# A convolution attention's weighted sums from 16-bit halves, with the rests made on GpSimd and VectorE

## The reference, cut to what is touched

```python
k = conv1x1(xA, wk, bk)      # (4, 128, 1024); v and q alike
attn = softmax(einsum('bcn,bcm->bnm', v, q), axis=2)
av = einsum('bcn,bnm->bcm', k, attn)
avw = einsum('oc,bcn->bon', wwg, av)
avw = (avw - bn1_m) * scale1 + bn1_b
o = conv1x1(avw, wout, bout)
o = (o - bn2_m) * scale2 + bn2_b
x = relu(o + xA)
# then: t = tokens(x); t += attention(layernorm(t)); t += experts(layernorm(t))
```

## Time and profile before

| | us |
|---|---|
| median of 3 runs | 1248.38 (1245.92 to 1252.49) |
| the profiled execution's own time | 1251.72 |
| its span, first to last instruction | 1249.9 |
| TensorE busy | 1120.8 (90%) |
| VectorE, ScalarE, GpSimd busy | 794.2, 634.3, 577.8 |
| granted TensorE clock, mean | 0.961 |

### The profile page before, as it was taken

How to read it: one execution, slowest core, us unless ns; L and a number is a source line. 1 busy time by engine, 2 the same in 40 slices (tenths; PEclk the granted TensorE clock), 3 DMA queues, 4 the chain that set the end, 5 groups by cost and what they waited for, 6 DMA issues and landing times.

```text
span 1249.9 us, 28738 instructions
## 1 busy us (share of the span) xinstructions
PE 1120.8 (90%) x10344; PEld 739.8 (59%) x10344; DVE 794.2 (64%) x1458; ACT 634.3 (51%) x1147; POOL 577.8 (46%) x461
## 2 busy tenths in 40 slices
PE   3999999975799999899989998689899999999993
PEld 1555555533344554454445444578799989998772
DVE  2666666655788888678768872666566555555540
ACT  0757575742477668666765675433233333333432
POOL 2425242413488761675276337256454444454420
PEclk9999999977799999999999999799999999999996
DMA  5235852544022230333243214623333233332228
GB/s 164 63 114 185 317 187 80 186 130 146 27 74 78 83 78 27 96 95 95 63 109 88 57 45 127 251 36 71 51 50 47 47 49 51 53 52 40 41 31 273
DMA packets 98854, 120.50 MB, mean 96 GB/s; under 512 B 29120, under 2 KB 76032, under 8 KB 98080
## 3 DMA queue, kind: packets, MB, share of 16 engines
q1 hardware_dynamic: 77744, 70.15, 19.0%
q0 software_dynamic: 20544, 42.22, 15.2%
q10 hardware_dynamic: 432, 6.29, 1.3%
HBM read 72.84 MB, written 45.60 MB: 95 GB/s over the span
## 4 chain that ended last, share of the span: by engine, by line
PE 80%; DVE 5%; DMA 4%; ACT 3%; issue 3%; SPq 1%; DVEq 1%; another core or an unknown queue 0%; POOL 0%; ACTq 0%; POOLq 0%
PE PP L945 25%; PE PP L1313 14%; PE PP L1201 9%; PE PP L1175 9%; PE PP L1029 4%; PE PP L1080 4%; PE PP L1126 3%; PE PP L1185 3%; PE PP L1190 2%; DVE mxp L1539 2%; PE PP L977 2%; DMA WB<-late_d 2%; ACT WB L872 1%; PE PP L1054 1%; PE PP L1280 1%
## 5 line engine op out<-in xcount | busy, mean ns | idle before, releaser
L872 ACT ACTIVATE WB<-PP 128x512 f32<-128x512 f32 x512 | 268.4, 604 | 174.8 <-PE PP L1201 174.8
L1539 DVE TENSOR_REDUCE mxp<-PP 128x2 f32<-128x1024 f32 x256 | 301.3, 1219 | 66.0 <-PE PP L1126 64.4
L916 ACT ACTIVATE WORK<-PP,b1c 128x256 f32<-128x256 f32 (+1 forms) x320 | 142.4, 450 | 266.0 <-PE PP L945 248.5
L945 PE MATMUL PP<-WORK,WB 128*128 128x256 f16 (+2 forms) x1984 | 221.1, 268 | 18.1 <-issue 9.7
L672 POOL TENSOR_TENSOR WB<-WB 128x1024 f32<-128x1024 f32 x80 | 188.9, 2361 | 78.2 <-PE PP L1190 69.4
L945 PEld LDWEIGHTS PP<-WORK,WB 128*128 (+1 forms) x1984 | 186.1, 103 | 49.2 <-issue 21.4
L728 POOL DMA_INDIRECT res_d<-WORK,lb x71 | 116.1, 1635 | 200.1 <-DVE WORK L1779 180.2
L1313 PE MATMUL PP<-WB,WORK 128*128 x1704 | 194.9, 273 | 0.0
L1313 PEld LDWEIGHTS PP<-WB,WORK 128*128 128x128 f16 x1704 | 164.4, 98 | 22.0 <-issue 0.9
L1201 PE MATMUL PP<-WORK 97*128 97x256 f16 x1024 | 159.3, 279 | 16.0 <-ACT WB L872 12.9
L638 POOL TENSOR_TENSOR WB<-WORK,WB 128x1024 f16<-128x1024 f32 x32 | 68.4, 2137 | 174.0 <-ACT WORK L778 173.9
(11 more groups left out here) (287 smaller groups left out, 1144.0 us busy)
## 6 DMA issues: line engine op xcount, KB each, us to landing
WORK<-in_L_ffn_W_dram POOLq DMA_DIRECT2D x32, 512.0 KB, 4.3
res_d<-WORK SPq DMA_DIRECT2D x8, 1024.0 KB, 4.5
late_d<-WB POOLq DMA_DIRECT2D x1, 6144.0 KB, 19.1
WB<-late_d ACTq DMA_DIRECT2D x3, 2048.0 KB, 14.8
v_d<-WORK SPq DMA_DIRECT2D x4, 1024.0 KB, 4.5
WORK<-q_hi_d SPq DMA_DIRECT2D x16, 256.0 KB, 3.6
WORK<-v_d SPq DMA_DIRECT2D x8, 512.0 KB, 5.8
WORK<-k_hi_d SPq DMA_DIRECT2D x16, 256.0 KB, 3.9
```

The source lines that it names most:

```text
L872: act.activation(PR[n % 3][:, c // 2, c % 2 * 2:c % 2 * 2 + 2], SCORES[m % 3] .rearrange("p (h n) -> p h n", h=2), ACT.Exp).then_inc(s("e_ ...
L916: act.activation(hid[:, k, 0:width], hidden_bank(k)[:, 0:width], ACT.Gelu, bias=b1c[:, bass.ds(e, 1), k], scale=1.0 / WSCALE)\
L945: mm = pe.matmul(dst, lhsT, rhs, start=(n == 0), stop=(n == len(pairs) - 1))
L1539: dve.tensor_reduce(mxp[:, n // 4 % 2, i, h:h + 2, k], PP[2 + h // 2][:, :].rearrange("p (h n) -> p h n", h=2), X_AXIS, ALU.max).then_inc( ...
```

## The change

- The exponential goes to `expo[i % 2]` in 32 bits. ScalarE waits for its own result and copies it to a 16-bit high half in `prob[i % 4][:, 0]` (semaphore hi_on). The rest, `expo - high`, goes to `prob[i % 4][:, 1]`: GpSimd makes it for blocks 0, 1, 2, 4, 5, 6, VectorE for 3 and 7.
- exp(i) waits for the rest of block i - 2; in batches 1 to 3 exp(0) also waits for the batch before's q and k stores to land.
- VectorE scales the row sum by 1/256, inverts it, makes the keys' high half and (scalar_tensor_tensor) their low half. S1 takes the 1/256 back.
- weigh(i) is three 16-bit products for each half of the columns instead of one 32-bit product, and waits for the rest.
- The weights: ScalarE splits part 0 after block 2, part 1 after block 7, parts 2 and 3 ahead of the layer norm's halves, and parts 4 to 7 after the units 0 to 3. GpSimd makes the rests of blocks 0 to 2 ahead of part 0's low half and those of 4 to 6 ahead of part 1's.

```diff
+KSCALE = 256.0
+REST_BY_VECTOR = (3, 7)
...
+        halved = "p (s n) -> p s n"
+        prob = [a.bitcast(F16).rearrange(halved, s=2) for a in prob]
...
+        expo = [QS[:, i * N:(i + 1) * N] for i in range(2)]
...
+            def low_exponentials(b, i):
+                pool.wait_ge(s("hi_on"), b * NT + i + 1)
+                if i >= 4:
+                    pool.wait_ge(s("av_made"), b * NT + (i - 3))
+                pool.tensor_tensor(prob[i % 4][:, 1], expo[i % 2], prob[i % 4][:, 0], ALU.subtract)\
+                    .then_inc(s("lo_pool"), 1)
+
             for i, (e, _, at, gap) in enumerate(parts):
+                for k in {0: (0, 1, 2), 1: (4, 5, 6)}.get(i % 8, ()):
+                    low_exponentials(i // 8, k)
...
             def tokens(b, last):
+                def rests(n):
+                    late = sum(i <= n for i in REST_BY_VECTOR)
+                    act.wait_ge(s("lo_pool"), b * (NT - 2) + n + 1 - late)
+                    if late or b:
+                        act.wait_ge(s("lo_dve"), b * 2 + late)
+
+                if b:
+                    act.wait_ge(s("st_q0"), FREE + b * 64)
+                    act.wait_ge(s("st_q1"), FREE + b * 64)
                 for i in range(NT):
                     act.wait_ge(s("max_kept"), b * NT + (i + 1))
+                    if i >= 2:
+                        rests(i - 2)
+                    act.activation(expo[i % 2], PP[i % 3][:, :], ACT.Exp, bias=nmax[:, i:i + 1],
+                                   accum_out=rsum[:, i:i + 1]).then_inc(s("exp_kept"), 1)
                     if i >= 4:
                         act.wait_ge(s("av_made"), b * NT + (i - 3))
-                    act.activation(prob[i % 4], PP[i % 3][:, :], ACT.Exp, bias=nmax[:, i:i + 1],
-                                   accum_out=rsum[:, i:i + 1]).then_inc(s("exp_kept"), 1)
-                    if i % 2 == 0:
-                        split_weights(b, i // 2)
-                split_weights(b, 4)
+                    act.wait_ge(s("exp_kept"), b * NT + i + 1)
+                    act.activation(prob[i % 4][:, 0], expo[i % 2], ACT.Copy).then_inc(s("hi_on"), 1)
+                    if i == 2:
+                        split_weights(b, 0)
+                split_weights(b, 1)
...
-                split_weights(b, 5)
+                split_weights(b, 2)
+                split_weights(b, 3)
...
-                    if u < 2:
-                        split_weights(b, 6 + u)
+                    split_weights(b, 4 + u)
...
                 def weigh(i):
-                    pe.wait_ge(s("exp_kept"), b * NT + (i + 1))
+                    pe.wait_ge(s("hi_on"), b * NT + (i + 1))
                     pe.wait_ge(s("ks_kept"), b * NT + (i + 1))
+                    if i in REST_BY_VECTOR:
+                        pe.wait_ge(s("lo_dve"), b * 2 + REST_BY_VECTOR.index(i) + 1)
+                    else:
+                        pe.wait_ge(s("lo_pool"), b * (NT - 2) + i + 1 - (i > 3))
...
                     for h in range(2):
-                        mm = pe.matmul(PP[3][:, h * HALF:(h + 1) * HALF], kTs[i % 4],
-                                       prob[i % 4][:, h * HALF:(h + 1) * HALF],
-                                       start=(i == 0), stop=(i == NT - 1))
+                        here = slice(h * HALF, (h + 1) * HALF)
+                        for n, (sk, sp) in enumerate(((0, 0), (0, 1), (1, 0))):
+                            mm = pe.matmul(PP[3][:, here], kTs[i % 4][:, sk], prob[i % 4][:, sp, here],
+                                           start=(i + n == 0), stop=(i == NT - 1 and n == 2))
...
                     dve.wait_ge(s("exp_kept"), b * NT + (i + 1))
+                    dve.tensor_scalar(rsum[:, i:i + 1], rsum[:, i:i + 1], 1.0 / KSCALE, None, ALU.mult)
+                    dve.drain()
                     dve.reciprocal(rinv[:, i:i + 1], rsum[:, i:i + 1])
...
-                    dve.tensor_scalar(kTs[i % 4], kT[:, i * P:(i + 1) * P], rinv[:, i:i + 1], None,
-                                      ALU.mult).then_inc(s("ks_kept"), 1)
+                    key = kT[:, i * P:(i + 1) * P]
+                    dve.tensor_scalar(kTs[i % 4][:, 0], key, rinv[:, i:i + 1], None, ALU.mult)
+                    dve.drain()
+                    dve.scalar_tensor_tensor(out=kTs[i % 4][:, 1], in0=key, scalar=rinv[:, i:i + 1],
+                                             in1=kTs[i % 4][:, 0], op0=ALU.mult, op1=ALU.subtract)\
+                       .then_inc(s("ks_kept"), 1)
+                    if i in REST_BY_VECTOR:
+                        dve.wait_ge(s("hi_on"), b * NT + i + 1)
+                        dve.tensor_tensor(prob[i % 4][:, 1], expo[i % 2], prob[i % 4][:, 0], ALU.subtract)\
+                           .then_inc(s("lo_dve"), 1)
```

More of the change, by code:

```diff
@@ L205, in hybrid_block @@
         qs = QS.bitcast(F16).rearrange("p (u s n) -> p u s n", u=2, s=2)
+        expo = [QS[:, i * N:(i + 1) * N] for i in range(2)]
         stage = take(2048).rearrange("p (u n) -> p u n", u=2)
-        kTs = [take(P) for _ in range(3)] + [SPARE[:, 3 * N:3 * N + P]]
+        kTs = [a.bitcast(F16).rearrange(halved, s=2)
+               for a in [take(P) for _ in range(3)] + [SPARE[:, 3 * N:3 * N + P]]]
         wqkv16 = take(1536).bitcast(F16).rearrange("p (s c n) -> p s c n", s=2, c=CC)
@@ L325, in s @@
             return S[name]
-        for name in ("q_low v_low ld_w ld_x0 ld_x1 ld_y0 ld_y1 bst_kept pool_const pe_prep dve_prep act_prep "
+        for name in ("q_low v_low ld_w ld_x0 ld_x1 ld_y0 ld_y1 bst_kept hi_on lo_pool lo_dve pool_const pe_prep dve_prep act_prep "
                      "q_made v_made k_made q_kept v_kept k_kept sc_made max_kept exp_kept ks_kept "
@@ L1394, in _ @@
             dve.tensor_tensor(vec[:, BE2:BE2 + 2], vec[:, BO:BO + 2], vec[:, BB2:BB2 + 2], ALU.add)
+            dve.tensor_scalar(vec[:, S1:S1 + 1], vec[:, S1:S1 + 1], 1.0 / KSCALE, None, ALU.mult)
             dve.wait_ge(s("pe_prep"), 2)
```

## The result

The changed kernel takes 1325.2 us in the median of four runs (1322.1 to 1327.7), the kernel before on the same chip 1249.1 (1245.9 to 1252.5): a ratio of 1.060, 95% interval 1.057 to 1.063, so it is 76 us slower. The direction was forecast; the time is 20 us above the 1305 and 3 us beyond the range.

The account below looks back on a forecast made before the run. TensorE, 90% busy, was taken as the bound; loops 23, ends of batches 0 and 2 7, batch 1 20 and batch 3 7 sum to 57 us on 1251.7: 1309, as a median 1305 us, range 1272 to 1322.

Parts of the forecast that it names:

- the later stages: Stages behind the convolution attention: taken as unchanged in length, 0 us.
- The new block chain: Block loops: exponential, 16-bit copy and rest, with a tail behind the last exponential, make each loop 1.0 us longer without collisions.
- the collisions: Block loops: VectorE's key instructions wait for GpSimd's subtractions on the shared port; with the chain +5.8 us a batch, +23 in all.
- +1.0, +4.0 and +5.8: Loss per batch loop in us: no collisions, low half slipping in ahead of GpSimd, or GpSimd going first (the one taken).
- rival 1: Block loops: no or fewer collisions, 4 x 1.0 instead of 4 x 5.8 us, 1286 us in all; chance 0.2.
- The weighted sums' gain: Block loops: six 16-bit matmuls take 1.29 us for 1.72, 13.8 us over four batches if TensorE stays the bound.
- The ends of batches 0 and 2: Part 6's late load delays unit 3 and k's store, whose landing holds exp(0): +3.5 us each, +7 together.
- the end of batch 1: SyncE's wait for the moved 6 MB store holds the q and k stores and so batch 2's exp(0): +20 us (16 to 22).
- Rival 3: TensorE's granted clock falls in the loops, slowing last weighted sums and output products: 5 x 4 = 20 us, 1325; chance 0.12.
- the rival's first term: At a loop's end, with the clock at 0.50, the last weighted sum costs 1.3 us more.
- the end of batch 3: Part 30's late load delays the 32nd low half, the next stage's operand loads and first matmul: +7 us (5 to 8).
- ScalarE's extra part ahead of the layer norm's halves: Ends of batches: one more weights' part on ScalarE, 1.9 us, costed at nothing as covered by TensorE's work after the loop.

Follow-up runs that it names:

- taking the lock away: Changed kernel with VectorE's two key instructions replaced by one-element reductions (row-sum division and keys' low half left out): 1306.6 us, 1.048.
- the four-block kernels with the lock gone: Kernel before with weights' parts spread, blocks 2 to 5 in halves, key instructions as one-element reductions, three places of the 6 MB store: 1.010, 1.018, 1.004.
- the halves alone: Changed kernel with the weights' parts back where the kernel before had them: 1313.6 us, 1.052.
- mending both its causes: Changed kernel with SyncE's 6 MB wait and fourth x's load behind batch 1's stores, 6 MB store behind the 16th part: 1302.1 us beside 1321.6.
- the run made to test it: Changed kernel with both 6 MB store and x's load moved later, and the last batch's part 3 split behind the layer norm's halves: 1299.5 us, 1.041.

## Why the prediction was right, and where it failed

The sum fell short in every stretch. The largest miss is a term put at nothing, the later stages (6.4 us); next come the ends of batch 1 (4.1) and batch 3 (3.2), each with steps of its own.

**Right, with its size.** The new block chain and the collisions: 27.5 predicted, 27.64 to 27.77 measured, each exponential within 0.3 us, and the cause is shown by taking the lock away (4 us back). The forecast's choice between +1.0, +4.0 and +5.8 rested on the earlier trace rows, where a 128-column scaling ended 0.09 us after GpSimd; it was the right one, and rival 1 falls. The weighted sums' gain appeared only in the four-block kernels with the lock gone.

**Right number, wrong cause.** The ends of batches 0 and 2 were put at 3.5 each, since the new wait for k's store would hold exp(0) until 107.3. They took 3.8 and 4.6. The step that failed is the store's landing, taken as 4.7 us after its issue: it took 2.6 and 2.7, and nothing waited for it. In batch 0 exp(0) waits for ScalarE's own stream: part 7's load and two instructions, v, and the exponentials' table, none of which was followed. The weights' move alone gives the same 44.9 us there without any wait for stores. In batch 2 it waits for the maximum and then the table. The store's wait is real elsewhere: 1.4 us over the maximum with the halves alone, 0.2 to 2.4 us in the kernels with x's load behind batch 1's stores, and 12.83 us beside the 6 MB.

**Too small, the end of batch 1: 20 for 24.1.** The chain was the right one up to ScalarE's third high half (SyncE's wait, the stores behind it), and it is shown: mending both its causes gives 19.5 us back. Counted from y1, unit 0's q store was to go out at 45.3 us and went at 46.9, since the 6 MB took 20.5 us for the 19.1 of the earlier trace rows. It was given 5.9 us and took 7.6, behind x's two loads. These two terms are 3.3 of the 4.1. From there to exp(0) the prediction had 10.2 us and it took 10.6, but by another chain: not unit 3's store, which landed at 205.8, but the slowed scores, the maximum (made at 206.65) and the table load. That was one of the prediction's own signs of being wrong, "if exp(0) of batch 2 waits for VectorE and not for a store". Rival 3 waved TensorE's idle off here, "but behind them exp(0) waits for stores"; it lay on the path with 1.3 us, and the table with 1.3 more, in place of the store's 5.1.

**Too small, the end of batch 3: 7 for 10.2.** The chain was the right one, part 30's load, part 31 and its low half. The load was to land 36.3 us after y1 at the latest (287.4 less 251.1), and ScalarE got it at 39.7:

```profile
348.90 1.06 ACT L792 ACTIVATE WB<-WORK 128x1024 f16<-128x1024 f32 x1 [4.15 <-DMA WORK<-in_L_ffn_W_dram]
```

The step that failed is a term put at nothing, ScalarE's extra part ahead of the layer norm's halves. Its low half falls into VectorE's layer norm and stretches it by 2.4 us (the collision again). Unit 0's high half, part 28's low half (31.9 us after y1 for the prediction's 29.6) and so the issue of part 30's load all stand 2.4 us later. The load itself took 5.4 us for the 4.3 of the earlier trace rows. This is read from the one trace; the run made to test it moved a load as well and doesn't separate the two.

**Missing, the later stages: 0 for 6.4.** "That stage is a chain from there on, so all of it stays" took the stages behind as unchanged. They are 963.6 us for 957.2, and 963.4 when the changed kernel was run again. Single executions of one kernel differ by up to 11 us here, so two times don't settle that; the place of the loss does. Counted from each stage's first maximum, VectorE's maxima fall 1.3 us behind the kernel before within 55 us, and 5.7 us by 140 us; at the end of the program it is 6.4.

```profile
360.40:365.40 5.00, 1.18 (x8) 0.17 (x8) 3.66 (x4) 0.00 (x0) 0.00 (x0) 0.50 0.99 320
```

Two kernels with no or four blocks in halves lose 1.2 to 1.3 us there too (it rises at 42.0 and 42.3), and four with all of them don't, so this part isn't bound to the halves. The other 4.4 us are. A load of v lands late, 5.8 us after its issue for 4.3; TensorE stands 2.38 us for 0.89, and the clock falls to 0.52 behind it. The kernel before, then the changed one:

```profile
417.58 0.83 PE L1201 MATMUL PP<-WORK 97*128 97x256 f16 x6 [0.89 <-DMA WORK<-v_d]
```
```profile
488.65 1.46 PE L1234 MATMUL PP<-WORK 97*128 97x256 f16 x6 [2.38 <-DMA WORK<-v_d]
```
```profile
486.50:488.50 2.00, 0.00 (x0) 0.00 (x0) 0.47 (x2) 0.00 (x0) 2.00 (x2) 1.00 1.09 354
488.50:490.50 2.00, 1.85 (x10) 0.84 (x10) 0.00 (x0) 1.15 (x3) 0.38 (x1) 0.52 0.57 171
```

The same six matmuls take 1.46 us for 0.83. All eight profiles of kernels with every block in halves have this wait at 1.8 to 2.5 us, and seven of them a stretch at the lower level behind it; they lose 1.0 to 4.4 us between 98 and 140 us of the stage. The other ten, the kernel before among them, have it at 0.8 to 1.0 with no such stretch, and lose 0.1 at most. Why the load lands later was not settled.

**Rival 3 gave 1325 and the time is 1325,** but not by its mechanism. The clock did fall in the loops: it is 0.94, 0.88, 1.00 and 0.94 in the four, where it was 1.00 before. Batch 1's:

```profile
115.21:142.89 27.68, 21.27 (x80) 7.91 (x78) 22.62 (x40) 21.65 (x28) 17.09 (x10) 0.88 0.23 73
```

But the loop at 1.00 is as long as the others (27.64 to 27.77), since TensorE is no longer what they wait for. Behind a loop's last weighted sum of the profiled run the output products take 3.70 us as before:

```profile
71.23 3.70 PE L973 MATMUL PP<-WORK 128*128 128x512 f32 x8 [0.91 <-DVE WORK L1511]
```

In two kernels run later batch 1's loop took 29.2 us instead of 27.7; in the changed kernel run again its last two weighted sums took 2.72 and 2.77 us for 1.3, so the rival's first term (1.3) can occur. Its 20 us didn't. That the totals agree is luck: the table of stretches tells the terms apart, the total doesn't.

**The range.** It left out most of rival 3 and took the later stages as certain. All misses over 1 us (1.6, 4.1, 1.1, 3.2 and 6.4) went up; a walk along a chain misses what it doesn't name, and here that was only ever added time: a table load, a stretched layer norm, a slower clock.

## What to carry to other kernels

A VectorE instruction of 0.3 us beside GpSimd's elementwise work costs what GpSimd has still to do, one or more of its instructions, and the next instruction of VectorE's stream pays for it. Before work is moved onto GpSimd, list what VectorE has of two SBUF inputs or two-port form in that stretch, however small.

Moved work takes its DMAs along: follow each one's issue past every queue it is moved behind, and ask which wait in that queue other stores stand behind. Here the moves alone cost 39 us in stretches in which nothing was computed differently.

A wait set ahead of an activation can cost time though it is fulfilled early: look where the table load stands, ahead of the waits or behind them.

A gain in one engine's busy time is worth only what the chain behind its last input leaves: 13.8 us were there by the count for eight blocks; four blocks gave 6.9 with the lock gone, and eight as the kernel stood lost 24.

## What the runs showed of the hardware

- A waiting VectorE instruction isn't always served at GpSimd's next boundary. In the changed kernel it got in after one of two rests (46.63 to 47.29, GpSimd's end at 47.21), and again between two instructions without a gap (to 51.88, at 51.80). In the halves alone it passed two such boundaries and waited for three instructions (51.10 for 5.49 us).
- A reduction over one element is a copy to 16 bits of 128 columns in 0.28 to 0.29 us that GpSimd's 4.31 us didn't touch; the scaling to 16 bits in its place took 0.66 and 0.83 us in the changed kernel and up to 5.49 with the halves alone.
- The exponentials' table load (1.28 us) stands ahead of the wait for the maximum where that is the only wait (99.71 and 103.84), and behind all the waits where two for stores are added (206.75 and 208.05). The second puts it on the path.
- After 21.3 us of idle TensorE ran its next six matmuls (128x512, 16-bit) at the lower level, at some 0.43 us each for 0.21. Elsewhere the clock fell behind stands of 2.0 to 2.4 us, in the loops (0.88 in batch 1's) and at v's load (0.52); behind one of 0.89 us there it stayed.
- One 6 MB store made stalls of 20, 12 or 21 us by its place alone: in front of batch 1's stores, beside k's, or ahead of x's load. It takes 19.1 us, and no engine but SyncE waits for it.
